# Four attention and expert layers on one core: one list of steps across layers in place of stages between barriers

## What is computed

```python
x = x + xattn_l(layernorm(x), ctx)     # l = 0..3; 16 heads of 8 columns
x = x + ffn_l(layernorm(x))

q, k, v = heads(xn @ Wq.T + bq), heads(ctx @ Wk.T + bk), heads(ctx @ Wv.T + bv)
s = q @ k.T / sqrt(8)
a = softmax(s)        # l = 0 (with a mask that is all ones), 1 and 3
a = sigmoid(s)        # l = 2
xattn = (a @ v) @ Wo.T + bo

w = route(xn @ Wr)    # weights of the two best of 8 experts; l = 0 with a capacity of 512
ffn = sum_e w[:, e] * ((silu(xn @ A_e) * (xn @ B_e)) @ C_e)       # l = 0, 1, 3
ffn = sum_e w[:, e] * (gelu(xn @ A_e) @ C_e)                      # l = 2
```

## Time and profile before

| | |
|---|---|
| median of three runs | 5229.23 us |
| profiled execution, its own time | 5252.85 us |
| its span | 5251.5 us |
| busy share of the span: PE, DVE, ACT, POOL | 84%, 63%, 69%, 0% |
| mean granted clock of PE | 0.883 |

### The profile page before, as it was taken

One profiled execution on the slowest core, in us unless ns is written; L12 is line 12 of the kernel. 1 busy time (PEld: TensorE's weight loads), 2 busy tenths in 40 slices (PEclk: granted clock), 3 DMA queues, 4 the chain that ended last, 5 costly groups with the idle time before them and its releaser, 6 DMA issues. The chain is left out here.

```text
span 5251.5 us, 70263 instructions
## 1 busy us (share of the span) xinstructions
PE 4416.7 (84%) x27838; PEld 1117.1 (21%) x27838; DVE 3322.2 (63%) x5918; ACT 3601.3 (69%) x3909; POOL 1.9 (0%) x6
## 2 busy tenths in 40 slices
PE   6888888887888889898878777778789889888877
PEld 2111111111521111111135311111262111111115
DVE  5789989882479988988624200001128998999824
ACT  5677777659257776766662599998736776777692
POOL 0000000000000000000000000000000000000000
PEclk7589999889858998988989899999895998999898
DMA  4100000000000000000000100000000000000000
GB/s 120 32 1 10 1 10 1 1 25 2 11 30 10 1 10 1 10 1 11 16 10 1 47 1 10 10 1 26 10 25 10 1 8 3 1 10 1 1 1 5
DMA packets 31156, 63.81 MB, mean 12 GB/s; under 512 B 6232, under 2 KB 24672, under 8 KB 28512
## 3 DMA queue, kind: packets, MB, share of 16 engines
q1 hardware_dynamic: 30816, 59.23, 4.7%
HBM read 45.57 MB, written 13.64 MB: 11 GB/s over the span
## 5 line engine op out<-in xcount | busy, mean ns | idle before, releaser
L722 ACT ACTIVATE prob<-scores 128x1024 f32<-128x1024 f32 (+1 forms) x2890 | 2890.4, 1072 | 917.3 <-PE scores L658 891.7
L754 DVE TENSOR_REDUCE mpart<-side 128x1 f32<-128x512 f32 (+1 forms) x4368 | 2602.5, 662 | 236.9 <-PE side L674 236.2
L686 PE MATMUL av<-prob,V_all 128*9 128x512 f32 x13056 | 1829.3, 634 | 257.0 <-ACT prob L722 256.9
L674 PE MATMUL side<-KB,QPb 32*128 32x512 f16 (+1 forms) x1248 | 396.8, 415 | 98.3 <-DVE mpart L754 61.9
L722 ACT ACTIVATE prob<-side 128x1024 f32<-128x1024 f32 x374 | 455.4, 1218 | 8.5 <-PE scores L658 8.5
L674 PE MATMUL side<-KA,QPb 32*128 32x512 f16 (+1 forms) x1248 | 391.1, 411 | 78.9 <-DVE mpart L754 67.4
L674 PE MATMUL side<-KB,QPa 32*128 32x512 f16 (+1 forms) x1248 | 386.5, 399 | 78.7 <-DVE mpart L754 66.7
L658 PE MATMUL scores<-QPa,KA 32*128 32x512 f16 x1496 | 336.9, 415 | 17.4 <-PEq L215 15.4
L686 PEld LDWEIGHTS av<-prob,V_all 128*9 128x9 f32 x13056 | 194.7, 89 | 706.3 <-ACT prob L722 547.0
L658 PE MATMUL scores<-QPa,KB 32*128 32x512 f16 x1496 | 330.4, 419 | 11.0 <-PEq L215 9.4
L658 PE MATMUL scores<-QPb,KA 32*128 32x512 f16 x1496 | 329.2, 404 | 1.8 <-ACT prob L722 1.8
(11 more groups left out here) (153 smaller groups left out, 2516.3 us busy)
## 6 DMA issues: line engine op xcount, KB each, us to landing
KA<-kparts SPq DMA_DIRECT2D x96, 100.1 KB
KB<-kparts SPq DMA_DIRECT2D x96, 100.1 KB
mstage<-in_mask SPq DMA_DIRECT2D x16, 400.2 KB, 3.3
Fin<-in_Fin SPq DMA_DIRECT2D x3, 2048.0 KB, 8.2
kparts<-hi SPq DMA_DIRECT2D x36, 128.0 KB, 1.7
kparts<-lo SPq DMA_DIRECT2D x36, 128.0 KB, 1.9
ctxT<-in_ctxT SPq DMA_DIRECT2D x2, 1024.0 KB, 8.8
Fout<-in_Fout SPq DMA_DIRECT2D x2, 1024.0 KB, 9.9
```

What stands on the lines that cost most here:

```text
L674: ins = pe.matmul(bank, QPn[rows(h), qt * P:(qt + 1) * P], Kmax[rows(h), chunk(c)], start=True, stop=not masked)
L686: ins = pe.matmul(AV[ROWS * h:ROWS * h + VC, :], V_all[0:n, kt, g * HG + h, :], prob[0:n, slot, (h % 2) * QB:(h % 2) * QB + QB], start=kt ...
L722: act.activation(prob[0:n, r % RING, :], pair.rearrange("p a b -> p (a b)"), ACT.Exp if softmax else ACT.Sigmoid, scale=SCALE).then_inc(se ...
L754: dve.tensor_reduce(mpart[:, qt, h, c:c + 1], MX[:, b, 0:chunk_of(c)], AX.X, ALU.max).then_inc(sem["side"], 1)
```

## The change

The program becomes one list of steps for all engines, `attention_steps`, with phases ordered layer, block, group (before: layer, group, block). A class `Order` counts the semaphores of the list, and each engine walks through its own steps. A unit `u` is one block of one layer, four phases. Beside the four phases of unit `u` the list places `finish_steps(u - 1)`: output projection, norm, router, all experts and next layer's queries of the other block. Beside the first block of a layer it places `kv_steps` of the next layer: keys and values are projected chunk by chunk from a ring of three chunks of the context, and the keys go to DRAM and back as stacks. Values have two buffers (VA, VB). Each background step has a slot, a quarter of a key tile, and `placed` puts the first matmul of an item that uses the score banks at slot 1. The maxima are spread by estimated costs of DVE (`COST`).

PSUM is dealt out anew: four banks of scores, used in turn as two pairs by scores, `up`, `kv` and `qproj`; two side banks; `av`; and one bank `misc` for what the background steps need. There is no third score pair in phases without maxima.

Other edits: `silu` is made of tanh, in the ACT pass `tanh` and copy `agc`, and gates on POOL (`gatea`, `gateb` of two instructions, `xk` once per expert; in layer 3 also `gatec`), or on DVE for units 3 and 7 (`by_dve`). The router's weights go into the operand (`xk`, `hscale`) by way of DRAM (`cwput`, `cwget`). `down` holds the expert's matrix still and moves 512 tokens, summing over experts in PSUM. The denominator of the softmax is spread by a matmul (`den`) and DVE takes a reciprocal of 128x512 (`norm`). Only layer 0 has the folded opening; its keys, values and the queries of both blocks come first in `opening_steps`. So the maxima of 23 phases are made beside other phases, where there were 21, and 9 phases are without, where there were 11. Two barriers are left in the attention part: after layer 0 and before the last unit's closing, which runs alone.

```diff
-        S = ctx.enter_context(nc.psum_tensor("scores", [P, 4, CH], F32))
-        MX = ctx.enter_context(nc.psum_tensor("side", [P, 3, CH], F32))
-        AV = ctx.enter_context(nc.psum_tensor("av", [P, CH], F32))
-        MISC = MX[:, 2, :]
+        S = ctx.enter_context(nc.psum_tensor("scores", [P, 4, CH], F32))
+        MX = ctx.enter_context(nc.psum_tensor("side", [P, 2, CH], F32))
+        AV = ctx.enter_context(nc.psum_tensor("av", [P, CH], F32))
+        Y = ctx.enter_context(nc.psum_tensor("misc", [P, CH], F32))
...
+    out = []
+    for c in range(NCH):
+        out.append((1, Step("SP", "ctx", (l, c))))
+        out.append((5, Step("PE", "kv", (l, c, 0))))
+        out.append((1, Step("PE", "kv", (l, c, 1))))
+        out.append((1, Step("PE", "kv", (l, c, 2))))
+        out.append((0, Step("ACT", "kvc", (l, c))))
+        out.append((0, Step("POOL", "ksplit", (l, c))))
+        out.append((8, Step("SP", "kput", (l, c))))
+    return out
+
+
+def norm_steps(u, tag):
...
+    LAG = 2
+    for i, (k, j) in enumerate(units):
+        if j == 0 and k + 1 < E:
+            out.append((0, Step("SP", "cwget", (u, lp, k + 1))))
+        if f["gated"]:
+            out += [(1, Step("PE", "up", (u, lp, k, j, 0))), (1, Step("PE", "up", (u, lp, k, j, 1))),
+                    (0, Step("ACT", "tanh", (u, lp, k, j)))]
+            if not by_dve(u, lp) or l == 3:
+                out.append((0, Step("ACT", "agc", (u, lp, k, j))))
+            if by_dve(u, lp):
+                out += [(0, Step("DVE", "gatea", (u, lp, k, j))), (0, Step("DVE", "gateb", (u, lp, k, j)))]
+            else:
+                out += [(0, Step("POOL", "gatea", (u, lp, k, j))), (0, Step("POOL", "gateb", (u, lp, k, j)))]
+            if l == 3:
+                out.append((0, Step("POOL", "gatec", (u, lp, k, j))))
+            if j == 0 and k + 1 < E and l != 3:
+                out.append((0, Step("POOL", "xk", (u, lp, k + 1))))
+            if i >= LAG:
+                down(i - LAG, 3)
+            else:
+                out.append((3, None))
...
+COST = dict(red=0.62, resid=0.7, sum=0.7, sumsq=0.7, yadd=0.7, norm=0.7, finc=0.7, fina=0.3, finb=0.2, routea=1.6, routeb=1.2,
+            routec=1.6, routed=0.4, gatea=0.7, gateb=0.7)
+Q = 4 * KT
+
+        mine = placed(base + 2, loads(u))
+        if b == 0 and l < 3:
+            mine += placed(base + (24 if u == 0 else 40), kv_steps(l + 1))
+        if u:
+            mine += placed(base + 12, finish_steps(u - 1))
...
+    for p in range(NG * units[0], last + 1):
...
+        total = len(ITEMS) * COST["red"] + cost_all
+        spent, done = 0.0, 0
+        for kt in range(KT):
+            for q in range(4):
+                at = p * Q + 4 * kt + q
+                if q in (0, 1):
+                    out.append(Step("PE", "score", (p, kt, q)))
+                    out.append(Step("ACT", "exp", (p, kt, q)))
+                if q == 2 and kt:
+                    out.append(Step("PE", "av", (p, kt - 1)))
+                if q == 2 and kt == 0 and p > NG * units[0]:
+                    out.append(Step("PE", "av", (p - 1, KT - 1)))
+                while n < len(back) and back[n][0] <= at:
+                    s = back[n][1]
+                    out.append(s)
+                    if s.eng == "DVE":
+                        spent += COST.get(s.what, 0.15)
+                    n += 1
+                if has:
+                    while done < len(ITEMS) and (kt >= KT - 2 or spent < total * (4 * kt + q + 1) / (Q - 8)):
+                        out.append(Step("PE", "max", (p + 1, done)))
+                        out.append(Step("DVE", "red", (p + 1, done)))
+                        spent += COST["red"]
+                        done += 1
+                    if kt == KT - 2 and q == 0:
+                        out += [Step("DVE", "fina", (p + 1,)), Step("DVE", "finb", (p + 1,))]
+                    if kt == KT - 2 and q == 3:
+                        out += [Step("PE", "flipmax", (p + 1,)), Step("DVE", "finc", (p + 1,))]
+    out.append(Step("PE", "av", (last, KT - 1)))
...
+            def item_free(what, *key):
+
+                n = o.slot[what, key]
+                if n >= 2:
+                    prev, k = o.items[n - 2]
+                    if prev == "score":
...
+            def side_bank(what, *key):
+
+                m = o.slot[what, key]
+                if m >= 2:
+                    wait_ge("red", m - 1)
+                return MX[:, m % 2, :]
+
+            for s in o.of("PE"):
...
+                    dve.reciprocal(oN[:, p % NG, :], MX[:, o.slot["den", s.key] % 2, :]).then_inc(sem["red"], 1)
...
-            finish(len(UNITS) - 1)
-
-        def ffn(l):
-            f = FFN[l]
-            if l < 3:
...
-                ffn_tensor(l, loop, first)
-                ffn_scalar(l, loop, variances, first + 1 + EXPD[l])
-                ffn_vector(v, l, loop)
-                barrier()
-                experts_tensor(l)
-                experts_scalar(l)
-                experts_vector(l)
-                dve.wait_ge(sem["yread"], QT * len(UNITS))
-                dve.tensor_tensor(state[:], state[:], yacc[:], ALU.add).then_inc(sem["vec"], 1)
-                barrier()
-            if l == 1:
-                dve.tensor_tensor(xs[:], xs[:], zs[:], ALU.add).then_inc(sem["vec"], 1)
-                barrier()
...
-        for l in range(4):
-            load_ffn(l)
-            if l < 3:
-                load_attn(l + 1)
-            attention(l)
-            ffn(l)
-        sp.dma_start(out.rearrange("(t p) d -> p t d", p=P), xs[:]).then_inc(d_out, 16)
-        sp.wait_ge(d_out, 16)
+            for name, n in o.count.items():
+                if name.startswith("d_"):
+                    wait_ge(name, n)
+
+        def run(steps):
+
+            o = Order(steps)
+            sync(o)
+            tensor(o)
+            scalar(o)
+            vector(o)
+            gpsimd(o)
+            barrier()
...
+        setup()
+        run(opening_steps())
+        first_sync()
+        first_tensor()
+        first_scalar()
+        first_vector()
+        barrier()
+        layer0 = attention_steps([0, 1])
...
+        with nc.If(n == P):
+            run(layer0)
...
+        run(attention_steps(range(2, 8)))
+        run(plain(finish_steps(7)))
```

More of the change, by code:

```diff
@@ L30 @@
 NCH = -(-KEYS // CH)
-VJ = -(-KT // 4)
 VC = DH + 1
@@ new lines, in softmax, with unit, phase, by_dve @@
+def softmax(l):
+    return l != 2
+def unit(u):
+    return u // 2, u % 2
+def phase(p):
+    return p // 8, p // NG % 2, p % NG
+def by_dve(u, lp):
+    return u in (3, 7)
+Step = namedtuple("Step", "eng what key")
+SEM_OF = dict(score="score", av="av", max="mx", flipmax="mx", den="mx", exp="exp", red="red", finc="red", norm="red")
+GROUP = dict(PE="bgP", ACT="bgA", DVE="bgV", POOL="bgG")
+DMAS = dict(kload=4, ctx=1, wexp=2, cwput=1, cwget=1, kput=3, wattn=5, wo=2, wffn=2, out=1)
+ITEM = ("score", "up", "kv", "qproj")
@@ new lines, in placed, with loads @@
+def placed(at, steps):
+    out = []
+    for gap, s in steps:
+        at += gap
+        if s is not None and s.eng == "PE" and s.what in ITEM and s.key[-1] == 0:
+            at += (1 - at) % 4
+        if s is not None:
+            out.append((at, s))
+    return out
+def loads(u):
+    l, b = unit(u)
+    out = []
+    if b:
+        if l + 2 < 4:
+            out += [(2, Step("SP", "wattn", (l + 2,))), (0, Step("DVE", "bqs", (l + 2,)))]
+        if l + 1 < 4:
+            out.append((0, Step("SP", "wo", (l + 1,))))
+        out.append((0, Step("SP", "wffn", (l,))))
+        if l == 3:
+            out.append((0, Step("DVE", "b1s", (l,))))
+    return out
@@ L101, with plain, opening_steps, __init__ @@
+def plain(steps):
+    return [s for gap, s in steps if s is not None]
+def opening_steps():
+    kv, qa, qb = kv_steps(0), finish_steps(-2), finish_steps(-1)
+    both = placed(0, qa) + placed(60, qb) + placed(6, kv)
+    both.sort(key=lambda x: x[0])
+    out = [s for at, s in both]
+    for p in range(2):
+        out += [Step("SP", "kload", (p, i)) for i in range(len(K_PIECES))]
+    out.append(Step("POOL", "fill", (0,)))
+    return out
 class Chain:
-    def __init__(self, engine, sem):
-        self.engine, self.sem, self.n = engine, sem, 0
+    def __init__(self, engine, sem, n=0):
+        self.engine, self.sem, self.n, self.first = engine, sem, n, n
@@ L187, in build @@
[L187 to L197 removed]
+        flat_sq = sq[:].rearrange("p t d -> p (t d)")
@@ L382, in open_tensor, with maxima_flip @@
                     max_product(qt, c, h)
-            finish_tensor(MX[:, 0, :], 2, n_max)
-        def finish_tensor(bank, before, read):
-            pe.wait_ge(sem["side"], read)
-            pe.wait_ge(sem["dvs"], before)
+            maxima_flip(n_max, 2)
+            pe.wait_ge(sem["mcnt"], 2)
+            pe.matmul(Y[:, 0:1], ones[:], mflag[:, 1:2], start=True, stop=True).then_inc(sem["counted"], 1)
+        def maxima_flip(reads, steps):
+            pe.wait_ge(sem["red"], reads)
```

(18 more changed lines are left out.)

1951 lines of the change are left out of this document (1035 added, 916 removed).

## The result

The changed kernel takes 6939.14 us (median of four runs, 6929.68 to 6955.44) against 5229.33 us for the kernel before. The ratio is 1.328, with a 95% interval of 1.323 to 1.334. The forecast of 5650 us had the sign and missed the size by 1289 us; the time lies outside the range. The profiled execution took 6948.46 us, 1274 more than the 5674 of the sum.

A forecast was written before the change was run, and what follows sets the result against it. It took phases with maxima to be bound by DVE at full clock, PE at half. Terms 3680, 860, opening 270, background 335 and 200, closing 88 and clock 240 made 5673, a median of 5650 us; range 5150 to 6250.

The forecast's parts named there:

- The stall: Key tiles with maxima: two side banks make a tile 3.04 us at full clock, 4.32 at half; 31 us a phase.
- Clock: 240: Half clock in some 18% of phases with maxima, as in the kernel before, losing 0.30 of each us: 240 us.
- Background in phases with maxima, 335: Half experts 220, keys and values 31, logits, flips and output projection 48, 24 denominators 36, on PE's path: 335 us.
- the 8.4 summed: Two tiles that a half expert has, 2 x 3.04 + 2.3 = 8.4 us, said to cover POOL's gates.
- my upper end: DVE's reciprocal of 128x512: 0.7 us taken, 8.2 if all paid by element, which adds 180 us.
- Phases without maxima: Nine phases at 95.5 us, 860, plus background 200; losing the third score pair costs nothing, ACT stays the cover.
- Closing: The last unit's closing alone: experts 42, projection, norm and router 40, output 5; 88 us, 131.5 before.
- opening: Layer 0's opening: 13 chained chunks 124, folded maxima 94, and the rest; 270 us, 196 before, 200 if chunks overlapped.
- POOL at nothing: POOL's gates cost nothing, covered by a half expert's two tiles; its 3.5 operations may take 2.4 us each.
- DVE stays the bound: Rival 1, phases with maxima: the stall is bridged and gone, 4985 us; chance 0.15.
- The second, full clock: Rival: the clock stays full because one list leaves no idle stretch at barriers, 5410 us; chance 0.12.
- The third: Rival: half clock in 13 phases without experts or keys, no matmul filling the array; 6350 us, half of them 6000; chance 0.17.

The follow-up runs named there:

- experiment 1: The kernel before, with its maxima in two of the three side banks in turn, nothing else changed: 6874 us, 1.330 times the kernel before.
- experiment 2: The changed kernel, with `misc` as a third side bank wherever no background step uses it for a while: 5821 us, ratio 1.122.
- experiment 6: On experiment 2's kernel: values split by queries 5688 us; both `up` halves ahead of values 5658; copy for reciprocal 5648; all three, division kept, 5525.
- experiment 5: The changed kernel on two side banks, values' block split by heads between the next PE steps: 9081 us; split by queries around a maximum: 6853 us.
- experiment 3: The changed kernel, with one more 128x512 fp32 matmul behind the values of 46 tiles in eight quiet phases: 6927 us, a single run.
- experiment 7: Experiment 2's kernel, with the experts' up and down matmuls moving 64 columns in place of 512: 5861 us against 5821.

## Why the prediction was right in sign and wrong in size

- **The stall.** Right to 0.03 us: 3.06 and 4.35 us a tile, for 3.04 and 4.32. Experiments 1 and 2 show that the bank is the cause.
- **"Clock: 240. It follows the trace."** This is the step that failed. I took the share of half clock from the kernel before (18%) and used it for a tile that PE works through differently. It was 71%, and the mean granted clock 0.70 in place of about 0.9. At a loss of 1 - 3.06 / 4.35 = 0.30, the 5326 us lost 5326 x 0.71 x 0.30 = 1120 us by this estimate, 880 more than the term. The clock was no surcharge beside the stall; it was the stall's larger half. Both tiles could be read from the earlier trace rows, and the phases before all came back to full clock within some 50 us, which I read as the chip's habit and not as that of a three-bank tile.
- **Background in phases with maxima, 335.** The remaining 190 of the 1071. Two tiles with half an expert took 9.57 us at full clock in phase 13 (from 3478.09 to 3487.66) for the 8.4 summed, in part since a large matmul between steps of other shapes takes 1.05 and not the 0.86 of a row of eight; 96 of them would make 112. The reciprocal took 3.36 us, 4.8 times the row of like shape that I took and under half of my upper end; 20 of them make 53 here. The other 25 are not placed.
- **Phases without maxima, 1060 against 1235.** Costed at nothing were the score banks: `up` holds a pair over the values, 3.9 us in phase 16 (from 4042.77 to 4046.66), and ACT waits (125 us busy of 212). Experiment 6 supports this by phases but mixes it with the shorter pass. The quiet ones were right: 98.5 us for 95.5.
- **Closing 92 for 88, opening 294 for 270.** Right, and near. The opening's chain of chunks was not tried apart.
- **POOL at nothing.** Right: 1.27 to 1.49 us for each gate of 128x512, under the 2.4 at which it decides. In layer 2 one operation of 128x1024 a half takes 2.36.
- **Rivals.** The one on the other side (DVE stays the bound) is excluded by experiment 1. The second, full clock, fell: in phase 2 PE waited 53 times for DVE, 0.8 us at the longest, and the clock was at half. The Trainium skill (TensorE: Matmul & The Clock Gate, "Loop structure matters more than you think") speaks of long waits; here short ones in every tile went with the loss. The third gave 6350 us for 13 phases at half clock, with 0.17; a quiet phase took 227 us for its 223, but there were ten. Its reason, that nothing fills the array, is not enough: experiment 2 brought the clock back with a third bank and experiment 5 with more small matmul time, neither with a matmul that fills it. It is not excluded as a part either: on two banks one large matmul a tile brought the clock back (experiment 3), and with an eighth of the experts' columns it was lost (experiment 7), though these matmuls still fill the array. Even the phases with experts and keys were at half clock for part of their time, which no rival had. The chances were wrong in that the forecast and this rival were treated as two cases, when the forecast's own stall, as experiments 1 to 3 show, went with it.

What stays open: what in the two-bank tile takes the clock down. The bank brings it about, and more work on PE undoes it, but a shorter stall did not (experiment 5), and no run added work with small matmuls in the quiet phases while the stall stayed as it was. Open too is why the phases with experts still need 230 to 280 us in experiment 6, and whether three banks for them too would bring the kernel under 5230 us. `misc` is in use there, and no kernel was tried that frees a bank. None of the kernels here beats the kernel before.

## To carry over

A ring of banks between two engines has to bridge the longest instruction block that stands in the producer's queue, here the values, and taking a buffer away must be priced at both of TensorE's clocks, with the clock as an outcome of the edit and not a constant of the kernel. Where a phase is at half clock, look first at what PE waits for; work that is hidden or left out may change nothing there, as the experts showed. The cheapest test for such a change is its one suspect edit in the old kernel: one digit at three places gave 1.33.

## What was not expected of the hardware

- Four heads' values in different strips of the output run side by side: eight instructions 1.05 us, two instructions of one head 1.02 us.
- TensorE stayed at half clock for 208 us on end (phase 2, from 733.6 to 941.8) with PE busy 88% of the time. With one more matmul of 1.06 us a tile the full clock came back, and it was lost 7 to 79 us behind the last of them.
- One long reading of a bank can hold the half clock: ten quiet phases took 1490 us with a reciprocal of 3.36 us near the start of nine of them, and 1368 with a copy of 0.69 in its place.
- A reciprocal on DVE takes 0.91 us for 128x128 and 3.36 us for 128x512, so most of it is paid by the element, where a reading or a copy of 128x512 takes 0.69.
